# Sixteen-head attention beside a gated feed-forward layer: the rows of the softmax maxima come from a transposing DMA

## The reference, cut to what matters

```
xn  = layernorm(x)                                  # over the 128 features
q,k,v = xn @ wq + bq, xn @ wk + bk, xn @ wv + bv    # 16 heads of 8 features
att = softmax(q @ k.T / sqrt(8)) @ v                # 256x256 scores for each head
ffn = sigmoid(xr @ W_r.T) * (relu(xk @ W_k.T)**2 @ W_v.T)
      # xr, xk: xn mixed with xn of the token before, by mu_r and mu_k
out = x + att @ wo.T + bo + ffn
```

## Time and profile before

| what | value |
|---|---|
| median of 3 runs | 470.46 us (470.16 to 470.57) |
| profiled execution, its own time | 470.89 us |
| span of its trace | 468.7 us |
| mean granted clock of TensorE | 0.978 |
| PE busy | 449.2 us (96%) |
| PEld busy | 271.7 us (58%) |
| DVE busy | 400.7 us (85%) |
| ACT busy | 390.2 us (83%) |
| POOL busy | 366.5 us (78%) |
| DMA | 60.43 MB, 44.9% of the 16 engines' span in the queue of the program |

### The profile page before, as it was taken

One profiled execution on the slowest core, in us unless ns is written; L12 is line 12 of the kernel. 1 busy time (PEld: TensorE's weight loads), 2 busy tenths in 40 slices (PEclk: granted clock), 3 DMA queues, 4 the chain that ended last, 5 costly groups with the idle time before them and its releaser, 6 DMA issues.

```text
span 468.7 us, 15677 instructions
## 1 busy us (share of the span) xinstructions
PE 449.2 (96%) x5254; PEld 271.7 (58%) x5254; DVE 400.7 (85%) x824; ACT 390.2 (83%) x865; POOL 366.5 (78%) x674
## 2 busy tenths in 40 slices
PE   5689999999989999999999999999999999999996
PEld 4245656556656556666665656566656666665554
DVE  7579989989988999899999999899998999989831
ACT  2038989989878998989899989889898989899884
POOL 6668888888878988788888888888888888887321
PEclk9569999999999999999999999999999999999999
DMA  4534355454445545344554544355544444455100
GB/s 137 154 115 142 100 140 162 127 154 133 111 132 148 157 127 153 108 131 132 146 158 129 155 139 126 105 144 155 158 134 138 137 124 122 140 151 146 50 15 24
DMA packets 86061, 60.43 MB, mean 129 GB/s; under 512 B 6224, under 2 KB 73808, under 8 KB 86032
## 3 DMA queue, kind: packets, MB, share of 16 engines
q1 hardware_dynamic: 86032, 60.06, 44.9%
HBM read 29.89 MB, written 29.36 MB: 126 GB/s over the span
## 4 chain that ended last, share of the span: by engine, by line
PE 87%; DMA 3%; issue 3%; ACT 2%; DVE 2%; SPq 1%; ACTq 0%; DVEq 0%; POOL 0%
PE bank_val L625 26%; PE bank_exp L701 19%; PE bank_max L711 10%; PE misc L730 4%; PE misc L752 4%; PE misc L640 4%; PE misc L659 3%; PE misc L741 3%; PE misc L793 3%; PE misc L786 3%; PE misc L667 2%; PE misc L767 2%; ACT probs L454 1%; PE misc L762 1%; DMA ops<-spill 1%
## 5 line engine op out<-in xcount | busy, mean ns | idle before, releaser
L551 DVE TENSOR_REDUCE neg_max<-bank_max 128x2 f32<-128x512 f32 x512 | 327.5, 683 | 40.5 <-PE bank_max L711 35.0
L454 ACT ACTIVATE probs<-bank_exp 128x512 f32<-128x512 f32 x504 | 272.8, 596 | 27.7 <-PE bank_exp L701 27.6
L711 PE MATMUL bank_max<-ops 48*128 48x256 bf16 x1024 | 163.7, 277 | 0.0
L701 PE MATMUL bank_exp<-ops 51*128 51x256 bf16 x1008 | 158.1, 272 | 5.5 <-issue 3.2
L625 PE MATMUL bank_val<-probs,val 128*25 128x256 f32 x2048 | 136.3, 384 | 0.8 <-ACT probs L454 0.8
L701 PEld LDWEIGHTS bank_exp<-ops 51*128 51x128 bf16 x1008 | 72.6, 94 | 72.5 <-issue 48.0
L625 PEld LDWEIGHTS bank_val<-probs,val 128*25 128x25 f32 x2048 | 50.4, 103 | 51.8 <-issue 26.3
L711 PEld LDWEIGHTS bank_max<-ops 48*128 48x128 bf16 x1024 | 74.9, 95 | 5.3
L356 POOL TENSOR_SCALAR xn<-x_in,moments,rstd 128x128 f32<-128x128 f32 x62 | 49.2, 801 | 0.0
L395 POOL TENSOR_TENSOR mixed_x<-mixed_x,xn_t 128x512 f32<-128x512 f32 x32 | 40.7, 1272 | 2.5
L370 POOL TENSOR_TENSOR qk_l<-qk_rest,qk_m 128x512 bf16<-128x512 f32 x31 | 36.0, 1162 | 2.5
(11 more groups left out here) (76 smaller groups left out, 619.7 us busy)
## 6 DMA issues: line engine op xcount, KB each, us to landing
ops<-spill SPq DMA_DIRECT2D x126, 192.0 KB, 3.4
spill<-qk_h SPq DMA_DIRECT2D x64, 192.0 KB, 3.4
spill<-qk_m SPq DMA_DIRECT2D x64, 128.0 KB, 1.9
x_in<-x SPq DMA_DIRECT2D x32, 128.0 KB, 2.2
spill<-qk_l SPq DMA_DIRECT2D x32, 128.0 KB, 1.8
y_out<-y SPq DMA_DIRECT2D x32, 128.0 KB, 1.9
ops<-shift SPq DMA_DIRECT2D x128, 6.0 KB
w<-weights SPq DMA_DIRECT2D x1, 448.0 KB, 3.0
```

The lines of the kernel that those rows point to most:

```text
L454: nc.scalar.activation(probs[g % 2][:, u % G, :, :], exp_bank(u, live)[:, :, :], ACT.Exp, scale=SCALE).then_inc(exp_done[u], 1)
L551: nc.vector.tensor_reduce(out=neg_max[hf][:, :, r, pr], in_=bank_max[MAX_BANK[v]][:, :, :], axis=AX_X, op=ALU.max, negate=True).then_inc(m ...
L701: exp_mm = nc.tensor.matmul(exp_bank(u, live)[:, i, :], ops[p][rows, hf, 1, pr, i * P:(i + 1) * P], ops[p][rows, hf, 0, pr, :], start=True ...
L711: max_mm = nc.tensor.matmul(bank_max[MAX_BANK[v]][:, i, :], of[rows, max_hf, 0, max_pr, i * P:(i + 1) * P], of[rows, max_hf, 1, max_pr, :] ...
```

## The change

`max_parts` is widened to 128 columns for each block of 128 queries (24 of them carry parts, the others are zeroed once at the start), and `shift` to 128 partitions x 2 x 128. A transposing DMA on SP takes the place of PE's two transposes, of ACT's copy and of the semaphore between them; the two DMAs that load `shift` into `ops` stay. On SP the transposing DMA of half 1 is put behind the load of x and ahead of the load of `ops`, half 1; that of half 0 behind the spill of the low parts and ahead of the load of `ops`, half 0. On POOL the split of half 0 moves ahead of rest. The bf16 identity goes. SP and POOL get one more set of counts in registers, ACT loses one.

```diff
-        max_parts = [sb(f"max_parts{i}", [P, ST, 2, 3, PR], BF16) for i in range(2)]
-        shift = [sb(f"shift{i}", [2 * 3 * PR, S], BF16) for i in range(2)]
+        max_parts = [sb(f"max_parts{i}", [P, ST, P], BF16) for i in range(2)]
+        shift = [sb(f"shift{i}", [P, ST, P], BF16) for i in range(2)]
...
+            def transpose_shift(half, count, before):
+                sp.wait_ge(parts_zero, 1)
+                sp.wait_ge(max_split[half], count)
+                after(sp, shift_in[half], before)
+                sp.dma_start_transpose(shift[half][:, :, :], max_parts[half][:, :, :].rearrange("p n c -> p (n c)")).then_inc(
+                    shift_done[half], 16)
+
+            def load_shift(half, p, done, before):
+
+                sp.wait_ge(shift_done[half], done)
                 after(sp, shift_in[half], before)
                 for r in range(2):
                     sp.dma_start(ops[p][RG * r + KS:RG * r + KE, half, 0],
-                                 shift[half][3 * PR * r:3 * PR * (r + 1), :]).then_inc(shift_in[half], 16)
+                                 shift[half][3 * PR * r:3 * PR * (r + 1), :, :]).then_inc(shift_in[half], 16)
...
                     load_x(t + 4, c)
+                if live(0):
+                    transpose_shift(1, n(0), moved(-1, 2))
                 if live(1):
 
                     after(sp, exp_scores[H - 1], n(-1))
...
                 if live(0):
-                    load_shift(1, p, n(0), moved(-1, 2))
+                    load_shift(1, p, moved(0, 1), moved(-1, 2))
                 if live(2):
                     spill_part(p, "m", qk_m, (m_done, m_done), n)
                     spill_l(p, n)
-
+                if live(1):
+                    transpose_shift(0, n(1), moved(0, 2))
+                if live(2):
                     after(sp, exp_scores[HALF - 1], n(0))
...
                 if live(1):
-                    load_shift(0, 1 - p, n(1), moved(0, 2))
+                    load_shift(0, 1 - p, moved(1, 1), moved(0, 2))
...
-            steps(sp, step, (2, SPILLS))
+            steps(sp, step, (1, 2, SPILLS))
...
+                if live(1):
+                    split_max(0, n(1), moved(0, 1))
                 if live(-1):
                     pool.wait_ge(ffn_done, n(-1))
...
-                if live(1):
-                    split_max(0, n(1), n(0))
...
-            def move_shift(half, bank, count, before):
-                act.wait_ge(shift_psum[half], count)
-                after(act, shift_in[half], before)
-                nc.scalar.copy(shift[half][:, :], shift_in_bank(bank)).then_inc(shift_done[half], 1)
...
-                    if u == 1 and live(0):
-                        move_shift(1, near, n(0), moved(-1, 2))
...
-                    if u == 9 and live(1):
-                        move_shift(0, far, n(1), moved(0, 2))
...
+            for i in range(2):
+                last = nc.vector.memset(max_parts[i][:, :, :], 0.0)
+            last.then_inc(parts_zero, 1)
...
-                nc.vector.tensor_copy(ident16[:, :], ident[:, :]).then_inc(consts_made, 1)
...
-            def transpose_shift(half, bank):
-                for st in range(ST):
-                    last = nc.tensor.transpose(shift_in_bank(bank)[:, st * P:(st + 1) * P],
-                                               max_parts[half][:, st].rearrange("p r j k -> p (r j k)"),
-                                               ident16[:, :])
-                last.then_inc(shift_psum[half], 1)
...
-                    if u == 1 and live(0):
-                        pe.wait_ge(max_split[1], n(0))
+                    if u == 3 and live(0):
                         pe.wait_ge(act_r_done, n(0))
                         after(pe, qk_rest_done[1], n(2))
-                        transpose_shift(1, near)
-                    if u == 3 and live(0):
-                        pe.wait_ge(shift_done[1], n(0))
...
-                    if u == 9 and live(1):
-                        pe.wait_ge(max_split[0], n(1))
+                    if u == 11 and live(1) and live(0):
                         after(pe, att_t_done, n(-1))
                         after(pe, qk_rest_done[0], n(2))
-                        if not live(0):
-                            pe.wait_ge(consts_made, 2)
-                        transpose_shift(0, far)
-                    if u == 11 and live(1) and live(0):
-                        pe.wait_ge(shift_done[0], n(1))
                         project_values(c + 1, far)
```

More of the change, by code:

```diff
@@ L91, in split_attention_ffn_kernel @@
         ident = sb("ident", [P, P])
-        ident16 = sb("ident16", [P, P], BF16)
         x_in = [sb(f"x_in{i}", [P, ST, D]) for i in range(TURN)]
@@ L144, in exp_bank @@
             return bank_exp[u % 2] if live(1) or u % 4 < 2 else bank_max[u % 2]
-        def shift_in_bank(bank):
-            return bank[0:2 * 3 * PR, 0:S // 2].bitcast(BF16)
         weights_in = sem("weights_in")
@@ L170, in split_attention_ffn_kernel @@
         max_split = [sem(f"max_split{i}") for i in range(2)]
-        shift_psum = [sem(f"shift_psum{i}") for i in range(2)]
+        parts_zero = sem("parts_zero")
         shift_done = [sem(f"shift_done{i}") for i in range(2)]
@@ L250, in load_first_ops @@
                         sp.dma_start(ops[p][RG * r:RG * r + KS, 0, :, pairs], src).then_inc(landed, 16)
-            def load_shift(half, p, count, before):
-                after(sp, shift_done[half], count)
+            def transpose_shift(half, count, before):
[6 more added lines that the diff above has]
+                sp.wait_ge(shift_done[half], done)
                 after(sp, shift_in[half], before)
@@ L327, in split_max @@
                 m, zero = neg_max[half], zeros[:, :, :, :]
-                part = [max_parts[half][:, :, :, j, :] for j in range(3)]
+                parts = max_parts[half][:, :, 0:2 * 3 * PR].rearrange("p n (r j k) -> p n r j k", r=2, j=3)
+                part = [parts[:, :, :, j, :] for j in range(3)]
                 last_unit = HALF * (half + 1) - 1
                 after(pool, max_done[last_unit], count)
-                after(pool, shift_psum[half], before)
+                after(pool, shift_done[half], before)
                 nc.gpsimd.tensor_tensor(part[0], m[:, :, :, :], zero, ALU.add).then_inc(max_h[half], 1)
@@ L409, in step @@
                 if live(1):
-                    split_max(1, n(1), n(0))
-            steps(pool, step, (SPILLS,))
+                    split_max(1, n(1), moved(0, 1))
+            steps(pool, step, (1, SPILLS))
         @block.scalar
@@ L488, in step @@
                         nc.scalar.activation(act_r[:, :], far[:, S:2 * S], ACT.Relu).then_inc(act_r_done, 1)
-            steps(act, step, (2, SPILLS))
+            steps(act, step, (SPILLS,))
         @block.vector
@@ L652, in project @@
                     after(pe, act_r_done, n(1))
-                elif live(1):
-                    pe.wait_ge(shift_done[0], n(1))
-                elif live(2):
+                elif live(2) and not live(1):
                     pe.wait_ge(val_done, n(2))
```

## The result

The changed kernel is slower: median 495.19 us (494.48 to 498.2, 6 runs) against 470.51 (469.73 to 471.64, 6 runs) for the kernel before; ratio 1.0535, 95% interval 1.0513 to 1.0557, +24.7 us. The profiled execution took 498.2, 3.0 above its median, with a span of 496.0.

A forecast was written before the change was run, and what follows sets the result against it. PE was taken as the bound, busy 14.00 of 14.00 us. Plain steps 8.6, turns 6.7, prologue 0.95 and end -0.4 gave +15.9 us, so 486.4 on the median; likely case 474 to 499, 8-in-10 range 466 to 530.

The forecast's parts named there:

- the forecast's formula: Whole kernel: 24 plain steps, 6 turns, prologue and end summed as functions of X; +15.9 us at X = 1.1.
- PE's saving: Between value mix and next scores: removing a transpose pair saves 0.1 us, 0.2 a step, 6.4 at most over 32 batches.
- X: SP issue time of one transposing DMA, ahead of the loads of ops, half 1: 1.1 us, likely 0.7 to 1.5.
- The transfer's price on the DMA engines: On the rings: 256 pieces of 256 B take 0.62 us over 16 engines, beside the issue, adding nothing.
- The plain step: Ring through SP and unit 6: larger of 13.18 and 12.64 + X; 24 steps add 8.6 us.
- The turns: Hardware loop turns: no slack at unit 6, X counts in full, 1.12 us each; 6 turns add 6.7 us.
- The other places: Ring transfer, half 1's shift rows, half 0 on SP and POOL's order: all hidden or with slack, nothing added.
- The prologue: Before the first step: transposing DMA ahead of the load of ops delays it by X - 0.15, 0.95 us.
- 1 (short issue): SP issue takes only 0.36 to 0.58 us; with 0.5 the time is 468.7 us. Chance 0.15.
- 2 (no ring): Load of ops forms no ring since SP reaches it earlier; full gain, 464.3 us. Chance 0.08.
- 4 (slow transfer): Transfer in 32-byte pieces takes 5.0 us on the rings, twice a step; 515 to about 610 us. Chance 0.13.
- Rival 3: Transposing DMA's landing, not issue, delays shift load and unit 8; over 3.5 us costs, about 524 us. Chance 0.14.

The follow-up runs named there:

- the one-block kernel: Changed kernel with each transposing DMA turning only the first of its two 128x128 blocks: 489.1 us, ratio 1.0428.
- the dose experiment: Kernel before plus useless SP issues between load of x and loads of ops, half 1: three plain DMAs 506.3 us, one transposing DMA 493.5 us.
- The control with earlier loads: Kernel before, nothing transposed by DMA, loads of ops, half 1, moved on SP to the end of the step before: 470.35 us, ratio 1.0004.
- the reordered kernels: Kernels transposing by DMA with SP's order around the loads of ops, half 1, changed against the changed kernel: 506.0, 502.0, 497.0 and, with one half only, 486.9 us.
- the control with the longer written-out part: Kernel before with the hardware loop starting at step 8 in place of step 4, four more steps written out: 470.1 us, ratio 0.9993.
- The changed kernel with the longer written-out part: Changed kernel with the hardware loop starting at step 8 in place of step 4, four more steps written out: 493.5 us, ratio 1.0467.
- half 1 alone: Only half 1 by transposing DMA, half 0 by PE and ACT; its ops loads and that DMA at the previous step's end, x loaded by ACT: 486.9 us.
- the kernels with the later transposing DMAs: Changed kernel with half 1's transposing DMA behind its ops loads on SP: 506.0 us; with both transposing DMAs issued by ACT behind units 1 and 9: 536.2 us.
- loads first: Changed kernel with the transposing DMA of half 1 behind the loads of ops, half 1, on SP: 506.0 us, ratio 1.0749.
- early loads: Changed kernel with the loads of ops and then transposing DMA of half 1 moved to the previous step's end, ahead of y's store: 502.0 us, ratio 1.0659.
- early loads with x on ACT: Changed kernel with half 1's ops loads and transposing DMA at the previous step's end, load of x issued by ACT behind unit 1: 497.0 us, ratio 1.0567.

## Why the prediction was right, and where it wasn't

The time fell in the range (466 to 530), slower, as forecast; 486.4 was forecast on the median and 495.2 measured. In the steady steps the mechanism was the one named: the issue of the transposing DMA on SP delays the loads of ops, half 1, and PE waits ahead of unit 6. That accounts for about half of the loss; the rest fell in the prologue and the first eight steps, which the sum had at 4.3 us in all and which cost 14.0. With the measured 1.33 in place of 1.1 the forecast's formula would have given 493.5, close to what came, but by luck: it would have had 17.4 us in the last 23 steps, where 13.4 came, and too little at the start.

- **PE's saving**: right. 1.00 us in place of 1.09 between mix and scores; no gain from ACT's lighter load shows.
- **X**: taken 1.1, measured 1.21, and 1.33 with the gap on SP (1.44 against 0.11). That 1.1 was near is in part luck: it was set between one and two shift loads by size, and the one-block kernel shows that size hardly enters (1.13 and 1.21 us). The comparison of the Trainium skill, "DMA: Bandwidth & Descriptors", by which a transposing issue on small tiles costs 1.23 times a plain one, is for transposes from HBM to SBUF and can't be carried over to this one from SBUF to SBUF: 1.21 against 0.4 us is a ratio of 3. The transfer's price on the DMA engines was overrated: 0.62 us of all 16 for a transfer, twice in each of 32 batches, would be 8% of the span, and their share rose from 44.9% to 46.3%, which is 19 us of all 16 or 0.30 a transfer.
- **The plain step**: forecast 12.64 + X, so 13.97 with the measured 1.33; measured 13.84 in the step shown and 13.91 in the median. The slope is as said (the dose experiment: 0.68 us of step for 0.65 us of dose), the slack at unit 6 was slightly larger than the 0.64 us read.
- **The turns**: the argument that X counts there in full because the load lands just when PE starts rested on one coincidence of two times, 254.0 and 254.09. The control with earlier loads gains at most 0.2 us a turn, so PE hardly waited for it. The term's size (6.7 us) was near what came: 14.23 and 14.71 us in the two steps around a turn, against 13.74 and 13.48, so 1.72 us for the pair where the forecast has 1.12 + 0.36. The additional set of counts costs SP 0.13 us a turn (1.82 against 1.69), estimated at 0.18.
- **The other places**: wrong. I had half 0 hidden. It costs some 7 us alone: half of that in the prologue, the rest in steps where PE waits at unit 14. Behind it stands a second ring over SP's later issues and unit 14, which the reordered kernels show bare.
- **The prologue**: forecast 0.95, measured 2.3. The transposing DMA took 1.39 us there, and the two loads behind it 1.72 in place of 1.19; PE waits 3.37 us for them in place of 1.29.
- **The start**: the mis-sized term. Here are the first matmuls of unit 3 in steps 0, 8 and 31, of the kernel before and of the changed one:

```profile
33.98 0.71 PE L730 MATMUL misc<-w,mixed_x 128*128 128x128 f32 x4
...
143.46 0.71 PE L730 MATMUL misc<-w,mixed_x 128*128 128x128 f32 x4
...
452.06 0.71 PE L730 MATMUL misc<-w,mixed_x 128*128 128x128 f32 x4
```

```profile
157.38 0.71 PE L719 MATMUL misc<-w,mixed_x 128*128 128x128 f32 x4
...
479.35 0.71 PE L719 MATMUL misc<-w,mixed_x 128*128 128x128 f32 x4
```

Step 0 stands at 36.23 after. So the prologue lost 2.3 us, the first eight steps 121.2 - 109.5 = 11.7, the other 23 steps 322.0 - 308.6 = 13.4, the end nothing; together the 27.3 us of the spans. For the 23 steps the forecast's terms give 18 x 0.36 + 5 x 1.12 = 12.1, near what came. For the first eight they give 3.3, and 11.7 came.

**What happens in the first eight steps.** The traces show most of it. Three of the eight steps lose 10.0 of the 11.7 us, and each goes the same way: something on SP is late, PE waits for it, and then the granted clock of TensorE falls from 1.00 to 0.50 for 3.4 us.

| step | late on SP (otherwise) | PE idle, ahead of | clock 0.50 from, to | step (before) |
|---|---|---|---|---|
| 3 | the two loads of ops, half 1, at 76.84 take 2.25 us (0.99) | 1.63 us, unit 6 | 83.69, 87.10 | 16.30 us (13.39) |
| 4 | a low spill lands after 4.2 us (2.0), and the loads of ops, half 0, follow at 103.08 | 1.86 us, unit 14 | 107.58, 110.99 | 17.97 us (14.32) |
| 6 | the transposing DMA at 123.84 takes 1.93 us (1.21) | 2.08 us, unit 6 | 131.48, 134.89 | 16.79 us (13.39) |

The waits, and the windows with the clock in the third column from the end:

```profile
82.36 0.27 PE L694 MATMUL bank_exp<-ops 51*128 51x256 bf16 x1 [1.63 <-issue]
...
107.09 0.27 PE L694 MATMUL bank_exp<-ops 51*128 51x256 bf16 x1 [1.86 <-issue]
...
130.34 0.27 PE L694 MATMUL bank_exp<-ops 51*128 51x256 bf16 x1 [2.08 <-issue]
```

```profile
83.69:87.10 3.41, 3.41 (x30) 1.24 (x30) 2.41 (x6) 2.10 (x5) 2.02 (x2) 0.50 0.50 138
107.58:110.99 3.41, 3.41 (x19) 1.80 (x20) 2.40 (x5) 2.66 (x6) 1.22 (x2) 0.50 0.55 153
131.48:134.89 3.41, 3.41 (x30) 1.55 (x27) 2.60 (x7) 2.29 (x5) 1.75 (x2) 0.50 0.52 137
157.38:479.35 321.97, 301.41 (x3612) 180.28 (x3610) 280.97 (x557) 266.63 (x569) 252.98 (x466) 1.00 0.49 137
```

In the kernel before the clock is 1.00 from 32.3 us to the end. The prediction named a granted clock below 1.00 as something that no term of its sum contains; it stays 1.00 in the steady steps, but not in these three. An estimate of the parts: PE waits 10.2 us in the first eight steps in place of 2.9, which is 7.3 more; three stretches at half clock cost at most 3 x 1.7 = 5.1; the transposes save 1.6. That makes 10.8 of the 11.7.

Why SP is late there: the trace of the changed kernel has eight code fetches of 16 KB between 60 and 152 us and none from there to 430. One overlaps the slow issue at 76.84, one the slow issue at 123.84, and one runs while the late spill is under way (100.67 to 102.14). It is hardly chance: between 34 and 430 us every issue on SP that takes over 0.3 us more than the median of its line, in the changed kernel and in the kernel before, overlaps such a fetch. Here is the queue line of the stretch:

```profile
q8 instruction: 8, 0.13, 0.6%
```

This fits that a fetch costs time only where a ring has no slack: the control with the longer written-out part has seven issues lengthened by 0.9 to 1.5 us and still takes 470.1. The changed kernel with the longer written-out part has such issues too, but in its first eight steps PE never waits over 1.25 us at a time, the clock stays at 1.00, and they take 112.3 us, 4.2 more than in its control, near the 3.3 of the forecast's terms. So the chain (fetch, late load, wait of PE, low clock) is read from the traces and no experiment sets it off on purpose. That the wait brings the clock down is argued from the order of events alone, and a wait of 1.6 us elsewhere in the changed kernel's trace has no fall behind it. The kernel with half 1 alone loses 10 us in its first eight steps with only one such low stretch, so there the waits weigh more.

Of the rivals, 1 (short issue), 2 (no ring) and 4 (slow transfer) are out: the issue is 1.21 us, PE waits ahead of unit 6 and the step grows with the dose, and the landing is 2.3 us. Rival 3 isn't what holds the changed kernel but stands right behind it, as the kernels with the later transposing DMAs show.

## What to carry to other kernels

An instruction that only issues a DMA has a price on its queue, and a queue that looks half idle can still be the bound: add up the issues between the event that starts the chain and the load whose landing PE needs, and compare the sum with the step. When such a chain has no slack, an issue that now and then takes longer costs in full, and more where the clock falls behind the wait. When one such chain is relieved, look for the next one on the same queue before giving a number: four of the reordered kernels here (loads first, early loads, early loads with x on ACT, half 1 alone) were mispriced for that. TensorE's transposes, at 0.1 us for two behind other matmuls, were far cheaper than an engine-free path that takes 1.2 us of a sequencer.

## What the runs showed of the hardware that I had not expected

- A transposing DMA, SBUF to SBUF, takes 1.13 us of the issuing queue for one 128x128 bf16 block and 1.21 for two, on SP; 1.19 on ACT. In the changed kernel it lands 2.3 us after its issue (median), right behind two loads of 192 KB 3.3 us.
- Plain DMAs of 128 partitions with 16 bytes each, SBUF to SBUF, take 0.6 us of SP each (1.82 for three), more than loads of 192 KB from HBM (0.4).
- On ACT the issue runs beside an instruction that has been started, and the next one waits for it: an issue from 303.29 to 304.64 has an exponential of 0.63 us starting inside it at 303.53, and ACT's next instruction starts at 304.68; an issue from 310.73 to 311.92 has one starting at 310.91, and the next starts at 311.96.
- An issue on SP that overlaps a code fetch of 16 KB can take 0.7 to 1.35 us longer than its line's median (four of them in the changed kernel between 40 and 152 us, at 55.92, 76.84, 123.84 and 148.49).
- The granted clock fell to 0.50 for 3.4 us at a time behind waits of PE of 1.63, 1.86 and 2.08 us, and each of these three steps was 2.9 to 3.7 us longer than the same step of the kernel before.
